# Attention scores in quarters of the array, eight heads in one group

## What is computed

```python
xn = _layernorm(x, gamma, beta)
w = sigmoid(xn @ Wx @ Ww + bw); k = xn @ Wk; v = xn @ Wv; r = sigmoid(xn @ Wr)
def step(state, inp):                    # per head, one token after another
    wt, kt, vt, rt = inp
    state = (1.0 - wt)[..., None] * state + kt[..., None] * vt[..., None, :]
    y = jnp.einsum('bhs,bhst->bht', rt, state)
    return (state, y)
attn = y @ Wo
x = _layernorm(x + attn)
x = _layernorm(x + moe(x))               # 12 experts of 320, the best two of each token
```

## Time and profile before

| | |
|---|---|
| time, median of 3 runs | 871.45 us (867.17 to 873.97) |
| time of the profiled execution | 866.74 us |
| its span | 864.9 us |
| mean granted clock of PE | 0.934 |
| PE busy | 736.8 us (85%) |
| DVE busy | 489.1 us (57%) |

### The profile page before, as it was taken

How to read it: one execution, slowest core, us unless ns; L and a number is a source line. 1 busy time by engine, 2 the same in 40 slices (tenths; PEclk the granted TensorE clock), 3 DMA queues, 4 the chain that set the end, 5 groups by cost and what they waited for, 6 DMA issues and landing times. The chain is left out here.

```text
span 864.9 us, 18399 instructions
## 1 busy us (share of the span) xinstructions
PE 736.8 (85%) x6073; PEld 522.8 (60%) x6074; DVE 489.1 (57%) x992; ACT 344.0 (40%) x718; POOL 328.2 (38%) x355
## 2 busy tenths in 40 slices
PE   5889999998999989999879752999999999999400
PEld 3657786967878768777646431656666666666200
DVE  4656867666676666767656466343434444343285
ACT  5455645455454454454564220222222222222154
POOL 0345544443345424554333004233333333433262
PEclk9999999998999989999989965999999999999855
DMA  8515335440454314543243094155455457222394
GB/s 341 219 58 170 110 106 147 147 136 30 132 147 147 114 36 147 147 143 102 72 125 99 0 352 181 39 182 178 154 203 186 175 185 275 86 85 86 121 341 157
DMA packets 38866, 126.73 MB, mean 147 GB/s; under 512 B 3984, under 2 KB 4368, under 8 KB 36496
## 3 DMA queue, kind: packets, MB, share of 16 engines
q1 hardware_dynamic: 31920, 103.31, 35.5%
q0 software_dynamic: 6880, 22.55, 7.7%
HBM read 81.02 MB, written 44.83 MB: 146 GB/s over the span
## 5 line engine op out<-in xcount | busy, mean ns | idle before, releaser
L831 DVE COPY_PREDICATED ST<-msk,pS 128x256 f32<-128x256 uint8 x224 | 121.1, 569 | 101.4 <-issue 67.2
L577 POOL TENSOR_TENSOR piece_parts<-piece,piece_parts 128x1024 f16<-128x1024 f32 x48 | 104.3, 2172 | 113.7 <-ACT piece_parts L523 113.7
L571 POOL TENSOR_TENSOR L<-L,AM 128x256 f32<-128x256 f32 x96 | 71.1, 741 | 118.8 <-ACT L L515 107.7
L1236 PE MATMUL pH<-ring,xgh 128*128 x344 | 103.8, 302 | 2.4 <-DVE xgl L1468 2.4
L1237 PE MATMUL pH<-ring,xgh 128*128 x344 | 103.7, 302 | 0.0
L1238 PE MATMUL pH<-ring,xgl 128*128 x344 | 103.7, 302 | 0.0
L299 PE MATMUL pS<-L 64*128 64x64 f32 x1536 | 98.4, 274 | 4.8 <-issue 4.8
L1553 POOL DMA_INDIRECT y_scratch<-ysb,sidx x43 | 42.9, 998 | 146.5 <-DVE ysb L1479 146.5
L299 PEld LDWEIGHTS pS<-L 64*128 64x128 f32 x1536 | 92.9, 191 | 5.1 <-issue 5.1
L1464 DVE TENSOR_TENSOR hid<-pH,sil 128x320 f32<-128x320 f32 x43 | 21.1, 492 | 114.6 <-ACT sil L1317 114.6
L555 DVE TENSOR_TENSOR L<-L,AM 128x256 f32<-128x256 f32 x96 | 70.6, 736 | 16.1 <-ACT L L502 9.9
(11 more groups left out here) (206 smaller groups left out, 1623.6 us busy)
## 6 DMA issues: line engine op xcount, KB each, us to landing
piece<-in_w_experts SPq DMA_DIRECT2D x48, 512.0 KB, 5.5
w_split_scratch<-piece_parts SPq DMA_DIRECT2D x48, 512.0 KB, 3.9
ring<-w_split_scratch SPq DMA_DIRECT2D x12, 2048.0 KB, 8.5
yin<-y_scratch SPq DMA_DIRECT2D x16, 512.0 KB, 6.1
x_scratch<-X SPq DMA_DIRECT2D x1, 4096.0 KB, 14.1
out_x<-X SPq DMA_DIRECT2D x8, 512.0 KB, 2.8
X<-in_x SPq DMA_DIRECT2D x1, 3072.0 KB, 22.8
X<-in_x SPq DMA_DIRECT2D x2, 512.0 KB, 7.2
```

The source lines that it names most:

```text
L571: g.tensor_tensor(next_kept(k, lv, 0), kept(key, k, lv, 0), by, ALU.mult).then_inc(k_dec, 1)
L577: g.tensor_tensor(piece_parts[buf][:, 1, :], piece[buf][:, :], piece_parts[buf][:, 0, :], ALU.subtract).then_inc(piece_lo, 1)
L831: v.copy_predicated(out[:, :, :, 0 if lv == 0 else 1, :], msk[:, lv, :, :].rearrange(shape, m=m), pS[:, :, lv * S:(lv + 1) * S].rearrange( ...
L1236: pe.matmul(p[:, 0, 0:F], xgh[par][:, k, :], wh, start=(k == 0), stop=False)
```

## The change

The scores of a chunk are worked out in one go for all eight heads. Keys and tokens of a chunk are each cut into halves of 64. Below the top level a token only meets keys of its own half, so `scores` multiplies, for each half f and head h, the 64 keys of that half with the 32 tokens of the level in the same half: a tile of 64 rows by 64 columns of the array that moves 32 columns. The top level, where tokens of the second half meet keys of the first, is cut into two pieces of 32 tokens. pS is viewed as `heads`: head i has 256 columns, of which level lv has 32. `mask` runs once a chunk, with seven masked copies and two plain ones, and it begins when all the scores are there. ST is one buffer instead of two. `apply_values` has two parts, with the first 64 keys (moving 128 token columns) and the last 64 (moving 64), and both stand behind `write_state`. ACT's copy of pY into yT is moved ahead of slot 3, with its norms. New semaphores are `pe_waited` (counted by PE, and waited for by none) and `y_half` (part 0 of the values is issued and done). The counts of the other semaphores change with it.

```diff
--- before.py
+++ after.py
@@ -41,7 +41,8 @@
 
 FIRST = [[2], [3], [4], [5], []]
 SECOND = [[6], [7], [8], [9], []]
-HALVES_OF = ((0, 1), (2, 3))
+HEADS = 2 * KT
+Q = S // 2
 GROUP = 4
 PIECE_AT = (4, 5, 6)
 
@@ -93,7 +94,7 @@
         w_o = sb("w_o", [P, KT, C])
         vecs = sb("vecs", [P, 3, KT])
         neg_bw = sb("neg_bw", [P, KT])
-        msk = sb("msk", [P, NMASK, 4, S], U8)
+        msk = sb("msk", [P, NMASK, HEADS, Q], U8)
         stats = sb("stats", [P, NT, 6])
         mv = sb("mv", [P, NT, 2])
         rstd = sb("rstd", [P, NT])
@@ -112,7 +113,7 @@
 
         AM = [sb(f"AM{m}", [P, 2, HP // (2 * m)]) for m in LEVELS[:-1]]
         dec_end = [sb(f"dec_end{i}", [P, 2, KT]) for i in range(2)]
-        ST = [sb(f"ST{i}", [P, 4, P]) for i in range(2)]
+        ST = sb("ST", [P, HEADS, P])
         kbT = sb("kbT", [P, C])
         yT = sb("yT", [P, KT, P])
         state = sb("state", [P, KT, P])
@@ -161,6 +162,8 @@
         s_dve = sem("s_dve")
         st_piece = sem("st_piece")
         waited = sem("waited")
+        pe_waited = sem("pe_waited")
+        y_half = sem("y_half")
         inter_done = sem("inter_done")
         st_used = sem("st_used")
         y_out = sem("y_out")
@@ -181,6 +184,7 @@
         norm2 = sem("norm2")
 
         block = ctx.enter_context(nc.Block())
+        heads = pS[:, :, :].rearrange("p b (i c) -> p (b i) c", i=2)
 
         def order(q, m):
 
@@ -278,25 +282,34 @@
                         i = pe.matmul(o, xl[par][:, kt, tok], wh["v"][:, kt, :], start=False, stop=(kt == KT - 1))
                 i.then_inc(a_full, 1)
 
-            def scores(n, k, half):
+            def scores(n, k):
 
 
                 pair, c = in_pair(k)
-                pe.wait_ge(s_dve, n * 2 + (half + 1))
+                if not isinstance(n, int) or n:
+                    pe.wait_ge(s_dve, n)
+                pe.sem_inc(pe_waited, 1)
                 b = k % 2
-                for g in HALVES_OF[half]:
-                    cols = slice(g * P, (g + 1) * P)
+                for g in range(KT):
                     for lv in range(NL + 1):
                         kl = max(lv - 1, 0) if lv != 1 else 1
-                        for h in range(2):
-                            rows = slice(h * S, (h + 1) * S)
-                            o = pS[:, 2 * (g % 2) + h, lv * S:(lv + 1) * S]
-                            if lv < 2:
-                                r_ = halves(rec[pair][rows, c, cols], 1)[:, :, lv, 0]
-                            else:
-                                r_ = halves(L[rows, (GROWN_AT[b] + (lv - 2)) if lv - 1 < TOP else TOP_AT[b], cols], LEVELS[lv - 1])[:, :, 1, :]
-                            k_ = L[rows, (KEPT_AT[b] + (kl - 1)) if kl < TOP else TOP_AT[b], cols] if kl else key[pair][rows, c, cols]
-                            i = pe.matmul(o, k_, r_, start=True, stop=True)
+                        for f in range(2):
+                            for h in range(2):
+                                rows = slice(h * S, (h + 1) * S)
+                                cols = slice(g * P + f * S, g * P + (f + 1) * S)
+                                if lv < 2:
+                                    r_ = halves(rec[pair][rows, c, cols], 1)[:, :, lv, 0]
+                                elif lv < NL:
+                                    r_ = halves(L[rows, GROWN_AT[b] + (lv - 2), cols], LEVELS[lv - 1])[:, :, 1, :]
+                                else:
+                                    r_ = L[rows, TOP_AT[b], g * P + S + f * Q:g * P + S + (f + 1) * Q]
+                                    cols = slice(g * P, g * P + S)
+                                if kl == 0:
+                                    k_ = key[pair][rows, c, cols]
+                                else:
+                                    k_ = L[rows, (KEPT_AT[b] + (kl - 1)) if kl < TOP else TOP_AT[b], cols]
+                                o = heads[f * S:(f + 1) * S, h * KT + g, lv * Q:(lv + 1) * Q]
+                                i = pe.matmul(o, k_, r_, start=True, stop=True)
                 i.then_inc(s_full, 1)
 
             def read_state(n, k):
@@ -310,16 +323,19 @@
                                   start=(g == 0), stop=True, skip_group_check=True)
                 i.then_inc(inter_done, 1)
 
-            def apply_values(n, k, half):
-
+            def apply_values(n, k, part):
                 pair, c = in_pair(k)
-                pe.wait_ge(s_dve, n * 2 + (half + 2))
-                for g in HALVES_OF[half]:
+                pe.wait_ge(s_dve, n + 1)
+                if part:
+                    pe.wait_ge(y_half, n + 1)
+                pe.sem_inc(pe_waited, 1)
+                rows, width = slice(part * S, (part + 1) * S), P - part * S
+                for g in range(KT):
                     for h in range(2):
-                        i = pe.matmul(pY[h * S:(h + 1) * S, 0, g * P:(g + 1) * P],
-                                      val[pair][:, c, g * P + h * S:g * P + (h + 1) * S], ST[half][:, 2 * (g % 2) + h, :],
+                        i = pe.matmul(pY[h * S:(h + 1) * S, 0, g * P + part * S:(g + 1) * P],
+                                      val[pair][rows, c, g * P + h * S:g * P + (h + 1) * S], ST[rows, h * KT + g, 0:width],
                                       start=False, stop=True, skip_group_check=True)
-                i.then_inc(st_used, 1)
+                i.then_inc(st_used if part else y_half, 1)
 
             def turn_keys(n, k):
                 pe.wait_ge(state_new, n + 1)
@@ -380,7 +396,7 @@
                 pe.wait_ge(r_kept, n * (NL - 2) + (NL - 2))
                 pe.wait_ge(k_dec, n * NL + (NL - 1))
                 pe.wait_ge(k_kept, n * (NL - 1) + (NL - 1))
-                scores(n, k, 0)
+                scores(n, k)
                 read_state(n, k)
                 turn_keys(n, k)
                 if slots is FIRST:
@@ -395,13 +411,12 @@
                     pe.sem_inc(m_full, 1)
                 if slots is FIRST:
                     fill(0)
-                apply_values(n, k, 0)
-                scores(n, k, 1)
                 fill(1)
                 write_state(n, k)
+                apply_values(n, k, 0)
                 fill(2)
+                apply_values(n, k, 1)
                 fill(3)
-                apply_values(n, k, 1)
                 fill(4)
 
             pe.wait_ge(consts_in, 32)
@@ -509,7 +524,7 @@
             else:
                 a.wait_ge(a_out, q * JOBS + 8)
                 if not isinstance(n, int) or n >= 2:
-                    a.wait_ge(s_full, n * 2 - 2)
+                    a.wait_ge(s_full, n - 1)
             if lv == TOP - 1 and (not isinstance(n, int) or n):
                 a.wait_ge(m_full, n * 3 - 2)
             a.copy(next_kept(k, lv, 1), kept(key, k, lv, 1)).then_inc(k_kept, 1)
@@ -542,7 +557,7 @@
             pair, c = in_pair(k)
             if lv == 0:
                 if not isinstance(n, int) or n >= 2:
-                    v.wait_ge(s_full, n * 2 - 2)
+                    v.wait_ge(s_full, n - 1)
                 v.tensor_tensor(next_grown(k, 0, 0), grown(rec, k, 0, 0), halves(dec[pair][:, c, :], 1)[:, :, 0, :], ALU.mult)
                 v.tensor_tensor(next_grown(k, 0, 1), grown(rec, k, 0, 1), AM[0][:, c, :].rearrange("p (b m) -> p b m", m=1),
                                 ALU.mult).then_inc(r_dec, 1)
@@ -560,7 +575,7 @@
             if lv == 0:
                 g.wait_ge(a_out, q * JOBS + 8)
                 if not isinstance(n, int) or n >= 2:
-                    g.wait_ge(s_full, n * 2 - 2)
+                    g.wait_ge(s_full, n - 1)
             else:
                 g.wait_ge(am_ready, q * NL + lv)
                 g.wait_ge(k_dec, n * NL + lv)
@@ -592,7 +607,7 @@
                 bank = m % 2
                 a.wait_ge(a_full, order(q, m) + 1)
                 if n is not None and m == 4:
-                    a.wait_ge(s_full, n * 2 + 2)
+                    a.wait_ge(s_full, n + 1)
                 if m < 2:
                     if m == 0 and not (isinstance(q, int) and q == 0):
                         a.wait_ge(x_lo, q)
@@ -718,13 +733,12 @@
                 split(2)
                 fill(2)
                 norms(2)
+                a.wait_ge(st_used, n + 1)
+                a.copy(yT[:, :, :], pY[:, 0, :].rearrange("p (g t) -> p g t", g=KT)).then_inc(y_out, 1)
                 fill(3)
                 norms(3)
-                a.wait_ge(st_used, n * 2 + 4)
-                a.copy(yT[:, :, :], pY[:, 0, :].rearrange("p (g t) -> p g t", g=KT)).then_inc(y_out, 1)
                 fill(4)
 
-            a.sem_inc(st_used, 2)
             a.sem_inc(y_out, 1)
 
             def root(i, step):
@@ -815,23 +829,26 @@
                 v.wait_ge(x_hi, q + 1)
                 v.tensor_tensor(xl[par][:, :, :], xf[:, :, :], xh[par][:, :, :], ALU.subtract).then_inc(x_lo, 1)
 
-            def mask(n, k, half):
-
-                v.wait_ge(st_used, n * 2 + (half + 1))
-                v.wait_ge(s_full, n * 2 + (half + 1))
```

(30 more changed lines are left out.)

## The result

The changed kernel takes 889.07 us (median of 4 runs, 884.9 to 890.19) against 870.25 us (867.17 to 873.97) beside it: 1.0206 times, 95% interval 1.0151 to 1.026. The forecast was 880, its range 828 to 905. So the change costs some 2%. The profiled execution has a span of 888.0 us against 864.9, 23.1 longer, and a mean granted clock of 0.899 against 0.934.

A forecast was written before the change was run, and what follows sets the result against it. PE's own instruction stream was taken to bound attention. +0.7 us a chunk x 14 = +10, jumps +2, tail -4 make +8: 875 us from the profiled 866.74, or 880 against the median; range 828 to 905.

The forecast's parts named there:

- case A: The forecast itself: quarters four abreast, instruction pauses, clock falling after most; 880 us, own range 866 to 895, chance .42.
- Scores at four abreast: PE's scores: four array quarters run at once, 3.6 us a chunk in place of 7.6, 4.0 less.
- D: Rival in the scores: quarters go two at a time; 876 us with clock held (chance .13), 905 if it falls (.12).
- Pause of 2.2 us a chunk: PE's scores: instructions outrun the fetch, so PE waits at the second block boundary, 1.6 to 2.7 us.
- Clock, +2.1 us a chunk: PE after pauses in the scores: half clock in three chunks of five, 2.1 us on average, between 0 and 3.4.
- The jumps, +1 us each: PE's two taken loop jumps: one more block boundary behind each, at half clock; 0 to 3 each, +2 in all.
- Masks at nothing: DVE's masks in crowded chunks: 4.0 us less work, worth 0 since PE doesn't wait for it.
- rival E: Rival: DVE's masks come late and PE waits 1 to 2 us in each chunk; around 890 us, chance .05.
- Values +0.4: PE's values in each chunk: two parts take 1.6 us together, where two pieces took 1.2.
- The tail, -4: Last chunk: copying yT ahead of the norms removes most of attend_out's 2.83 us wait and some low clock; 0 to -5.
- Rival B: Pauses in PE's scores but the clock holds, with work on both sides of each; 850 us, chance .14.
- Rival C: No pauses in PE's scores, as instruction fetch keeps up; 825 us, chance .14.

The follow-up runs named there:

- e8_pause22: The kernel before, with bounds assertions on two loads and 22 semaphore increments on PE amid the first half of each chunk's scores: 941.74 us, 1.0835.
- e6_yt_back: The changed kernel with bounds assertions on two loads and ACT's copy of pY into yT put back behind slot 3 and its norms: 895.25 us.
- e2_half: The changed kernel with bounds assertions on two loads, leaving out scores of the second half of keys and tokens (output not the reference's): 839.83 us, 0.9676.
- c1_after: The changed kernel with only bounds assertions added on two loads in the experts' part, the base for reading the experiments: 892.73 us, 1.0269.
- e9_order_unroll: The changed kernel with bounds assertions, scores in two lots, DVE's masks behind low_x and levels 1 and 2, and PE's loop written out: 839.32 us, 0.9648.

## Why the prediction was right, step by step

The direction and the main mechanism were right, and the forecast was 9 us too low, half of the whole move of 18.8. Between the profiled executions +8 was forecast and +23.1 came. The range of case A, 866 to 895, holds the result, but it does not follow from the bounds that it names: -4.0 + 1.6 + 0.4 + 0.6 = -1.4 and -4.0 + 2.7 + 0.4 + 3.4 = +2.5 us a chunk, times 14 and less 2, give 850 and 904 us.

Scores at four abreast: 3.6 us forecast, 58 ns a set or 3.7 us a chunk measured. Right, and D is out.

Pause of 2.2 us a chunk (1.6 to 2.7): 28.2 us away from the jumps in 14 chunks, 2.0 a chunk. Right in the mean, and wrong in its shape: it is 0.4 to 1.3 us or 2.0 to 3.3. The step that took the packet's delay as one figure between 3.4 and 4.5 us is the one to correct; entry to use is 3.0 to 4.0 us in eight of the 15 and 4.6 to 5.6 in seven. The long ones all have busy DMA engines, but so have some of the short ones, so what decides between the two stays open.

Clock, +2.1 us a chunk: chunks 0 to 12 lost 28.6 us against 6.9, and 13.8 of these stand behind the two jumps. That leaves 15 for eleven ordinary chunks, 1.3 each. Over-sized, since a short pause mostly left the clock alone (six of the seven lone pauses under 1.4 us); for a pause of 2.1 us in every chunk e8_pause22 gives 2.6.

The jumps, +1 us each: under-sized. The clock behind them cost (13.8 - 6.8) / 2 = 3.5 us more each, and the pauses about one jump were 2.70 and 2.00 us where the same place had 2.50, since the next boundary comes soon behind the first. Writing out the loop gives 20 to 25 us after, and 10 to 14 before, so the jumps and what they set off cost at least 6 us more than before, where I had put 2. The new places of the block boundaries are in that difference too.

Masks at nothing: right in the crowded chunks; the waits for X behind them are 2.3 us in all, in the last three chunks. So rival E, whose 890 us lies nearest to the result, has the number and not the cause. Values +0.4: their parts last 1.09 and 0.68 us on the timeline (503.24 and 508.18), where each half lasted 0.66: +0.45.

The tail, -4: wrong in sign, and the largest miss, +11.3 measured. The step that failed is "with the copy ahead of the norms most of the wait goes". The wait for yT is 3.01 us after and 2.83 before, and e6_yt_back shows that the copy's place does nothing. In its place came waits for ACT of 15.8 us where they were 9.1, and 3.1 us of pauses with a lower clock. e2_half parts the two: its scores last as long and have no pause in the tail, its waits for ACT there are the same to 0.2 us, and its tail takes 88.3 us (378.81 to 467.09, clock 0.85) against 93.5 in c1_after. So pauses and clock are about 5 us of the tail's growth, and the waits for ACT about 6. Why ACT is waited for longer is read from the rows and not shown by a run: before, DVE began the masks earlier and so the norms' sums, and PE had scores to run while ACT normed.

Against the sum: in chunks 0 to 12 I had +0.7 x 13 + 2 = +11, and 10.6 came; in the tail -4, and +11.3 came. The first agreement is luck: it rests on two errors that cancel, a clock term too large and a jump term too small. That the result lies in the range at all is owed to the range's width, as the tail was missed by 15 us.

Rival B (pauses, but the clock holds) falls by the clock of 0.92 in chunks 0 to 12 and by e8_pause22. Rival C (no pauses) falls by the 37.3 us of them. e2_half, with half of the work left out, and e9_order_unroll, with 5.6 us of pauses and 13.3 of waits for X, come nearest to it, at 839.8 and 839.3 us, where I had put 825.

The two rules of the Trainium skill. "Runtime: NRT & Kernel Launch", Instruction fetch mechanics: blocks of 256 instructions agree with the five chunks that have two pauses (128 matmul records apart); that dispatch is slower than the fetch does not hold here, with 37.3 us of pauses, since quarters of the array run through a block in 1.9 us. "TensorE: Matmul & The Clock Gate", Wait — 56ns, not 53.3ns?: starts never closer than about 25 ns does not hold for tiles on different quarters, 14.6 ns on average here; starts on one and the same tile are 58 ns apart.

## What to carry to other kernels

Smaller tiles bring more instructions for the same work, so count instructions per microsecond and not only array time: where a stretch runs through 256 of them in less than the fetch of a block takes (3 to 6 us here), it pauses, and the pause can cost as much again in clock. Break such a stretch in two with slow work between, then look at which engine waits for the later end, and move its waiting instruction behind the work that others need first. An edit that is a loss as it stands (1.02) can be a gain with these two (0.965), and a program's tail, where engines take turns, wants a reckoning of its own.

## What was not expected of the hardware

From the entry of a block to the instruction packet it took 0.6 to 1.3 us or 2.1 to 3.3 us. The DMA share of the stretch was 0.58 to 0.98 with the second, and anything from 0.00 to 0.99 with the first, so that the packets queue behind data is likely and not shown. From packet to use it took 2.2 to 2.7 us at either. Pauses of 2.1 us in a full stream were enough to bring TensorE's clock down to its lower level, at an average of 2.6 us of clock time each. Semaphore increments in a row started 150 ns apart on PE, though a record of one lasts 51 ns. A loop of three rounds on PE cost some 10 to 14 us of 870, by its two jumps.
